# Layer 1 of a two-layer transformer kernel: KV times the gated output weights, z on the queries, gate and spread matrices on GpSimd

## The reference

```python
Q = relu(proj(Wq, bq)) * decay        # decay = exp(-pos / n)
K = relu(proj(Wk, bk)) * decay
V = proj(Wv, bv)
KV = einsum('bhnd,bhne->bhde', K, V)  # 32 x 32 for each head
Ksum = K.sum(axis=2)
Z = 1.0 / (einsum('bhnd,bhd->bhn', Q, Ksum)[..., None] + EPS)
out = einsum('bhnd,bhde->bhne', Q, KV) * Z
x = x + ga * (out @ Wo.T + bo)
```

## Time and profile before

| | |
|---|---|
| time, median of 3 runs | 2087.24 us (2083.95 to 2090.82) |
| profiled execution, its own time | 2086.4 us |
| its span | 2084.5 us |
| PE busy | 1964.7 us, 94% |
| DVE busy | 1078.9 us, 52% |
| ACT busy | 639.0 us, 31% |
| POOL busy | 439.6 us, 21% |
| mean granted clock | 0.976 |

### The profile page before, as it was taken

How to read it: one execution, slowest core, us unless ns; L and a number is a source line. 1 busy time by engine, 2 the same in 40 slices (tenths; PEclk the granted TensorE clock), 3 DMA queues, 4 the chain that set the end, 5 groups by cost and what they waited for, 6 DMA issues and landing times. The chain is left out here.

```text
span 2084.5 us, 25631 instructions
## 1 busy us (share of the span) xinstructions
PE 1964.7 (94%) x10088; PEld 1399.4 (67%) x10088; DVE 1078.9 (52%) x1876; ACT 639.0 (31%) x1152; POOL 439.6 (21%) x385
## 2 busy tenths in 40 slices
PE   6999999999999997699999999997998969999998
PEld 4677545554545545578888888886885658888886
DVE  4456876666766715743434434336335665434334
ACT  3231445455555563322111111113221231111111
POOL 0122766666544365000000000000003000000000
PEclk9999999999999999899999999999999989999999
DMA  9753421422421003020000000002000011100002
GB/s 316 227 154 115 93 52 42 93 56 49 108 47 29 5 2 132 23 74 31 31 1 31 31 31 1 1 1 89 6 6 31 1 41 41 31 21 21 6 0 81
DMA packets 61720, 111.86 MB, mean 54 GB/s; under 512 B 6000, under 2 KB 21248, under 8 KB 61568
## 3 DMA queue, kind: packets, MB, share of 16 engines
q1 hardware_dynamic: 54144, 85.05, 14.2%
q0 software_dynamic: 7456, 25.18, 4.0%
HBM read 84.77 MB, written 25.44 MB: 53 GB/s over the span
## 5 line engine op out<-in xcount | busy, mean ns | idle before, releaser
L446 DVE TENSOR_REDUCE part_max<-banks 128x1 f32<-128x512 f32 (+2 forms) x640 | 357.3, 613 | 156.4 <-PE banks L418 96.6
L917 ACT ACTIVATE probs<-banks 128x512 f32<-128x512 f32 (+3 forms) x640 | 310.7, 538 | 282.7 <-PE banks L844 141.1
L418 PE MATMUL banks<-kst,qst 96*128 96x512 f32 (+2 forms) x640 | 261.6, 417 | 12.1 <-DVE part_max L446 9.2
L840 PE MATMUL banks<-qst,kst 98*128 98x512 f32 (+2 forms) x640 | 251.7, 413 | 0.2 <-ACT probs L917 0.2
L1384 DVE TENSOR_TENSOR tokens_a<-banks,tokens_a 128x512 f32<-128x512 f32 x224 | 151.5, 688 | 73.5 <-PE banks L210 71.9
L1409 DVE TENSOR_TENSOR tokens_b<-banks,tokens_b 128x512 f32<-128x512 f32 x64 | 44.3, 692 | 267.6 <-ACT tokens_b L1330 267.6
L208 PE MATMUL banks<-h_hi,f_wg_hi 128*128 128x512 f32 x432 | 170.4, 394 | 12.4 <-DVE f_wg_lo L1348 12.4
L208 PE MATMUL banks<-f_d_hi,f_hid_hi 128*128 128x512 f32 x432 | 171.7, 398 | 5.9 <-issue 3.6
L209 PE MATMUL banks<-h_lo,f_wg_hi 128*128 128x512 f32 x432 | 170.1, 394 | 0.0
L210 PE MATMUL banks<-f_d_hi,f_hid_lo 128*128 128x512 f32 x432 | 169.9, 393 | 0.0
L210 PE MATMUL banks<-h_hi,f_wg_lo 128*128 128x512 f32 x432 | 169.7, 393 | 0.0
(11 more groups left out here) (188 smaller groups left out, 3268.7 us busy)
## 6 DMA issues: line engine op xcount, KB each, us to landing
tokens_a<-in_L_wmod SPq DMA_DIRECT2D x12, 1024.0 KB, 7.1
qst<-q_hi SPq DMA_DIRECT2D x32, 256.0 KB, 6.0
kst<-k_hi SPq DMA_DIRECT2D x32, 256.0 KB, 8.1
x<-in_L_attn_x SPq DMA_DIRECT2D x4, 1024.0 KB, 13.2
q_hi<-qk_out_hi POOLq DMA_DIRECT2D x16, 256.0 KB, 3.0
q_lo<-qk_out_lo POOLq DMA_DIRECT2D x16, 256.0 KB, 3.4
k_hi<-qk_out_hi POOLq DMA_DIRECT2D x16, 256.0 KB, 4.1
k_lo<-qk_out_lo POOLq DMA_DIRECT2D x16, 256.0 KB, 4.4
```

The costliest lines, as they stand in the source:

```text
L418: mm = nc.tensor.matmul(dst[:, 0:wide], qst[n % QS][0:BIASROW, h, P * t:P * t + P], kst[(NB * g + c) % KS][0:BIASROW, h, 0:wide], start=Tr ...
L446: nc.vector.tensor_reduce(part_max[:, n % 2, ht, c:c + 1], max_bank(slot)[:, 0:wide], AX_X, ALU.max).then_inc(max_read, 1)
L840: mm = nc.tensor.matmul(dst[:, c0:512], kst[ck % KS][0:BIASROW + 2, h, at:at + P], qst[n % QS][0:BIASROW + 2, h, c0:512], start=True, stop ...
L917: nc.scalar.activation(probs[:, q % PS, h, c0:512], score_bank(sh)[:, c0:512], ACT.Exp, scale=SCALE).then_inc(exp_done, 1)
```

## The change

The output weights are gated by POOL, at the end of its list in the QKV block, once both loads have landed. In the next block kv is transposed by PE (4 transposes into bank 6) and copied by ACT, and each of its four tiles is multiplied with a chunk of the gated weights (4 plain fp32 matmuls into banks 2 to 5). These merged weights are split into w_hi (ACT) and w_lo (DVE). The spreads of z then multiply the queries themselves, and the projection of the scaled queries with the merged weights gives the attention output. The 16 numerators and their 16 copies are gone, and so are DVE's four gate multiplications. The four spread matrices are made by POOL, ahead of its bias additions. DVE makes the first w_lo after z and the other three after the fourth attend.

```diff
             gated = sem(ctx, tag + "w_gated_s")
...
+            merged = sem(ctx, tag + "merged")
...
+                def bias_vector(dve):
+                    dve.wait_ge(bias_loaded, 16)
+                    nc.vector.tensor_tensor(bias_row[:], bias_row[:], gate, ALU.mult).then_inc(bias_gated, 1)
+
+                def merged_tensor(pe, k, left):
+                    nc.tensor.matmul(bank[2 + k][:], left, raw[:, k, :], start=True, stop=True).then_inc(merged, 1)
+
+                def merged_scalar(act):
+                    for k in range(KT):
+                        act.wait_ge(merged, k + 1)
+                        nc.scalar.copy(w_hi[:, k, :], bank[2 + k][:]).then_inc(w_hi_s, 1)
+
+                def merged_vector(dve, ks):
+                    for k in ks:
+                        dve.wait_ge(w_hi_s, k + 1)
+                        nc.vector.tensor_tensor(w_lo[:, k, :], bank[2 + k][:], w_hi[:, k, :], ALU.subtract).then_inc(w_ready, 1)
...
# the QKV block, POOL, after its four w_lo
+                        pool.wait_ge(early_loaded, OUT1)
+                        for k in range(KT):
+                            nc.gpsimd.tensor_tensor(early_square[:, k, :], early_square[:, k, :], early_gate[:], ALU.mult)
...
# the output-projection block
+                def zb_bank(i):
+                    return bank[6 + i % 2][:]
                 def zb_step(pe, i):
                     b, g = divmod(i, G)
-                    dst = use_bank(pe, ("zb", i))
                     if i == 0:
                         pe.wait_ge(z_step, 4)
                         pe.wait_ge(spread_ready, NB)
+                    elif i >= 2:
+                        pe.wait_ge(at_ready, i - 1)
...
                 def attend(dve, i):
                     b, g = divmod(i, G)
                     dve.wait_ge(zb_mm, i + 1)
-                    dve.wait_ge(num_copied, i + 1)
                     here = at[:, g, 512 * b:512 * b + 512]
-                    nc.vector.tensor_tensor(here, bank_of(("zb", i)), here, ALU.mult).then_inc(at_ready, 1)
+                    nc.vector.tensor_tensor(here, zb_bank(i), here, ALU.mult).then_inc(at_ready, 1)
...
# POOL
+                        pool.wait_ge(spread_loaded, 32)
+                        for b in range(NB):
+                            nc.gpsimd.tensor_scalar(spread[:, b, :], pattern, of_block[:, b:b + 1], None,
+                                                    ALU.mult).then_inc(spread_ready, 1)
                         out_p.bias_gpsimd(pool)
...
# PE
+                        for g in range(G):
+                            last = nc.tensor.transpose(bank[6][:, P * g:P * g + P], kv[:, g, :], ident[:])
+                        last.then_inc(kv_turned, 1)
                         for g in range(G):
                             for b in range(NB):
...
                         last.then_inc(den_mm, 1)
-                        for kind, i in events[:G * (NB + 1)]:
...
+                        for g in range(G):
+                            if g == 0:
+                                pe.wait_ge(kv_copied, 1)
+                            out_p.merged_tensor(pe, g, kv_t[:, P * g:P * g + P])
+                        for i in range(G):
+                            zb_step(pe, i)
                         on_tensor(pe)
...
# ACT
-                        out_p.weights_scalar(act)
-                        for i in range(G * FIRST):
-                            numerator(i)
-                        for i in range(G * FIRST, G * NB):
-                            numerator(i)
+                        act.wait_ge(kv_turned, 1)
+                        nc.scalar.copy(kv_t, bank[6][:]).then_inc(kv_copied, 1)
+                        out_p.merged_scalar(act)
                         out_p.hi_scalar(act, 0)
                         on_scalar(act)
...
# DVE
-                        out_p.weights_vector(dve)
-                        dve.wait_ge(spread_loaded, 32)
-                        for b in range(NB):
-                            nc.vector.tensor_scalar(spread[:, b, :], pattern, of_block[:, b:b + 1], None,
-                                                    ALU.mult).then_inc(spread_ready, 1)
+                        out_p.bias_vector(dve)
                         dve.wait_ge(den_mm, 1)
...
+                        out_p.merged_vector(dve, range(0, 1))
                         for i in range(G):
                             attend(dve, i)
+                        out_p.merged_vector(dve, range(1, KT))
                         out_p.lo_vector(dve, 0)
```

More of the change, by code:

```diff
@@ L1695, in build_program @@
                 z_step = sem(ctx, "z_step")
-                num_mm = sem(ctx, "num_mm")
-                num_copied = sem(ctx, "num_copied")
+                kv_turned = sem(ctx, "kv_turned")
+                kv_copied = sem(ctx, "kv_copied")
                 zb_mm = sem(ctx, "zb_mm")
@@ L1704, in build_program @@
                             mod_cols[:, 1, CB, :], h2_hi, h2_lo, zbufs=1)
[L1707 to L1710, removed]
+                pattern, z_sum, kv_t = (norm.z[:, 0, i, :] for i in range(3))
+                def zb_bank(i):
+                    return bank[6 + i % 2][:]
                 def zb_step(pe, i):
                     b, g = divmod(i, G)
-                    dst = use_bank(pe, ("zb", i))
                     if i == 0:
@@ L1718, in zb_step @@
                         pe.wait_ge(spread_ready, NB)
[L1719 to L1733, removed]
+                    elif i >= 2:
+                        pe.wait_ge(at_ready, i - 1)
+                    nc.tensor.matmul(zb_bank(i), spread[:, b, P * g:P * g + P], z_hi[:], start=True, stop=False)
+                    nc.tensor.matmul(zb_bank(i), spread[:, b, P * g:P * g + P], z_lo[:], start=False, stop=True).then_inc(zb_mm, 1)
                 def attend(dve, i):
@@ L1782, in _ @@
                     def _(act):
-                        def numerator(i):
-                            b, g = divmod(i, G)
-                            act.wait_ge(num_mm, i + 1)
-                            nc.scalar.copy(at[:, g, 512 * b:512 * b + 512], bank_of(("num", i))).then_inc(num_copied, 1)
-                        out_p.weights_scalar(act)
-                        for i in range(G * FIRST):
-                            numerator(i)
-                        for i in range(G * FIRST, G * NB):
-                            numerator(i)
+                        act.wait_ge(kv_turned, 1)
+                        nc.scalar.copy(kv_t, bank[6][:]).then_inc(kv_copied, 1)
+                        out_p.merged_scalar(act)
                         out_p.hi_scalar(act, 0)
@@ L1809, in _ @@
                         nc.vector.tensor_tensor(z_lo[:], z_sum, z_hi[:], ALU.subtract).then_inc(z_step, 1)
+                        out_p.merged_vector(dve, range(0, 1))
                         for i in range(G):
                             attend(dve, i)
+                        out_p.merged_vector(dve, range(1, KT))
                         out_p.lo_vector(dve, 0)
-                        dve.wait_ge(spread_ready, NB)
-                        dve.wait_ge(z_step, 4)
                         on_vector(dve)
```

## The result

The changed kernel takes 2069.85 us (median of four, 2068.76 to 2072.13) against 2086.12 beside it: ratio 0.992, 95% interval 0.9901 to 0.994. Run again on another occasion it gave 0.9932 (0.9918 to 0.9945). So it is 0.7 to 0.8% faster, some 14 to 16 us. The forecast was 6.6 us, and the range ended 4 us short of the result: the sign was right, the size was not. One execution ran apart, the profiled one of e7 (2385.81 us at a mean granted clock of 0.77 from beginning to end), and is left out of every comparison.

What follows compares the result with a forecast made beforehand. PE bounds long stretches of the QKV block and after 1760; at the output-projection start engines wait for each other. -10.4 there and +3.8 in the QKV block give -6.6 on 2086.4: 2079.8, median forecast 2080.6 us, range 2074.0 to 2088.5.

Steps and rivals of the forecast that it cites:

- Where the gain is made: Output-projection block: first projection, held by late z, numerators and ACT's order, starts at 1614.0 against 1624.38, gaining 10.4 us.
- point 2: Output-projection block: z starts at 1598.8, not 1602.39, keeps its 6.84 us beside POOL and is complete at 1605.6.
- point 1: Output-projection block: transposes ahead of the denominators move their end later by 0.5 us (0.4 to 1.0), to 1598.7.
- the loss in the QKV block: POOL's gate multiplications hold DVE 4.3 us; 3.2 reach PE, plus 0.6 for the clock: 3.8 us lost (0 to 6).
- Points 3 and 4: Output-projection block: four merged products (3.7 us) cost nothing; POOL's spreads, 1.3 us each, end at 1602.3, 3.3 in hand.
- Point 5: Output-projection block: first spread matmul to end of fourth attend takes 4.5 us (3.9 to 5.2), ending at 1610.2.
- Point 6: Output-projection block: w_lo until 1612.0, then c_lo 1.2 us plus 0.65 lost to POOL; the product starts at 1614.0.
- The cover of 1.07 us on ACT: QKV block: slack between the first key tile's end at 1450.26 and L182 on ACT at 1451.33, taken off DVE's delay.
- The 0.6 us for a falling clock: QKV block: 0.6 us added because PE's clock may fall after its 3.2 us standstill.
- the question of proportion or turns: QKV block: DVE slowed in proportion beside POOL (3.0 us lost) or held for whole POOL instructions (4.3 taken).
- Rival C: Output-projection block: POOL's spread matrices set the start; deciding from 2.1 us each, 0.3% slower (2093.6) at 5.4; chance 0.08.
- its lowest case: Gate multiplications don't reach PE and the output-projection gain is at its 11.6 us bound: 2075.6, with run spread 2074.0.

Runs made afterwards that it cites:

- e7: Changed kernel with POOL's four gate multiplications taking one input (a gate column; weights not gated rightly): 2072.13 us, ratio 0.9931, three executions.
- the square: Block start to first projection: before 32.4 us, merged weights alone (e2) 26.8, spreads on POOL alone with additions held back (e6) 26.8, both (changed kernel) 18.3.
- e2: Changed kernel with the four spread matrices made by DVE again: 2079.28 us, ratio 0.9963.
- e3: Kernel before with one part of the change alone, the four spread matrices made by POOL: 2082.76 us, ratio 0.9989, not told from no change.
- e4: Changed kernel with POOL's four gate multiplications held back until the items of two token blocks have been read: 2072.83 us, ratio 0.9938.
- e7b: The kernel of e7 run again for an undisturbed profile: 2071.15 us, ratio 0.993.
- e8: e1 with the bias gated and added to x by POOL in the QKV block, behind the items DVE has read: 2068.76 us, ratio 0.9917.
- e1: Changed kernel with the output weights gated by DVE at the start of the output-projection block, not by POOL in the QKV block: 2071.12 us, ratio 0.993.
- a2: The changed kernel itself run once more: 2071.45 us, ratio 0.9932.
- e6: e3 with POOL's bias additions held back until the second c_lo is done: 2078.32 us, ratio 0.9961.
- e9: e8 with eleven matmuls nobody reads, one ahead of the first spread and ten ahead of the first projection: 2068.10 us, ratio 0.9914.
- e8b: The kernel of e8 run again, on the same chip as a2: 2069.31 us, ratio 0.9925.

## Why the prediction was right or wrong

**Where the gain is made** was right: the first projection hung on the late z, the numerators and ACT's order, and the square shows that the first two carry 14.1 us together. What failed is the price of three terms: the length of z (point 2), its start (point 1) and the loss in the QKV block.

**Point 1, the denominators.** I moved their end by 0.5 us to a later time; it came earlier. z started 5.75 us after the block's start, not 6.8. The same 16 calls took 3.64 (e2) to 6.23 us (e3), by how long the clock was at 0.50 in them; in e2 it stayed at 1.00. It goes with the length of the QKV block: where that was 173.2 or 173.3 us the denominators took 3.6 to 4.65 us, where it was 170.7 to 171.2 us they took 5.0 to 6.2 (13 profiles). So some 1.2 us of what POOL's gates cost PE came back as clock: the denominators ended 5.7 us after the block's start, and 6.9 in e4, e7b and e8. With the longer z this is why e4 won nothing. In e1 they ended only 0.2 us later than in the changed kernel; there it was z, the spreads and c_lo. That the two are linked is seen in all these profiles; why is not shown.

**Point 2, the length of z**, is the step that failed, with the largest error of the block. I kept 6.84 us "since POOL works beside it as before"; it took 5.27, 1.6 us less. The 6.84 holds only if POOL's additions are beside z's last two instructions, the cast and the rest. By my figures they would have been: spreads done 10.3 us after the block's start, the cast at 10.9. In fact the spreads cost 1.55 each on POOL, not 1.3, and ended at 10.8, and z, early, had its last two instructions from 9.9 to 11.0. Both errors were needed for it: either alone leaves an addition beside one of the two at the least. In e1 and e4, where the additions began before z_lo, z took 6.6 and 6.4.

**Points 3 and 4**: the merged products cost nothing, and the spreads were done at 1604.03, before z was complete at 1604.22. That was luck to 0.2 us, as I gave them 3.3 us in hand.

**Point 5, the spreads and attends**, was sized for a low clock (4.5 us) that did not come: from 1604.27 to 1606.55 + 1.29 = 1607.84 are 3.6. In a2 the clock did fall in them and they took 4.1. **Point 6**: 3.6 us from the fourth attend to the projection against 3.8 forecast. The first c_lo took 1.84 us, as forecast (1.85), but e3 shows that the bound was wrong: a starved c_lo took 7.14 us. It wasn't in my range at all and would have cost 5 us.

These terms sum up the 3.7 us between 22.0 and 18.3: 1.05 + 1.6 + 0.9 + 0.2.

**The QKV block** was forecast at +3.8 us and took +2.1. The mechanism was right, and e1, e4 and e7b bear it out: POOL delays DVE, and DVE's late z delays L182 on ACT and so PE. The term that was too large is DVE's delay, and a part that I added was not there. The two w_lo and the decay products lost 2.0 + 0.8 us, and the L195 ahead of them 1.0, which I hadn't counted; z ended 3.65 us later (counted from the block's first transposes, 1427.99 before and 1427.07 after), not 4.3. The cover of 1.07 us on ACT held: L182 came 2.49 us later, 1.2 less than z. PE lost it in three places, 1.07 at L195, 0.77 and 0.5 at the transposes, not in one idle of 3 us. The 0.6 us for a falling clock did not come. Some 0.3 us came back between the blocks, where PE's wait fell from 2.73 to 2.39; so it did in e4, whose QKV block of 170.7 us puts the price of the gates at 2.5 us. Why that wait is shorter is not shown.

On the question of proportion or turns, where I cited the Trainium skill's page "SBUF — State Buffer", section "Who interferes with whom": the 3.65 us lie between the 3.0 and the 4.3 of the two ways, and do not decide it. The times of e3 agree with a port that is held for whole instructions. They disagree with the page's rule that whoever issues first gets it, since four additions that started after c_lo had begun its 7.14 us went ahead of it; here the measurement decides.

**Rival C** did not come: 1.55 us each is below the 2.1 from which it decides. But with z complete at 11.0 us and the pattern there at 4.6, it would have decided from 1.6 on. The Trainium skill's "GPSIMD Engine Reference", section "4.1 Engine selection", led the other way: one-input work was dearer than the two-input addition (1.27), not cheaper.

**The rest** of the 14.2 us between the spans, and of the 16.3 between the medians, lies in stages that the change didn't touch, and the range left it out. The feed-forward part took 375.9 to 378.2 us over these kernels. In all of them PE stands still for 2.21 us once near its end, and in some the clock falls behind that. Stretches of the 11 us behind it, before and then after (length, PE busy, clock, DMA share, GB/s):

```profile
2043.09:2054.09 11.00, 11.00 (x41) 0.84 0.01 1
```

```profile
2031.60:2042.60 11.00, 11.00 (x48) 1.00 0.01 1
```

41 matmuls against 48 are 7 x 0.23 = 1.6 us. e6 and e9 look like after there, e3, e8 and a2 like before; as a2 is the changed kernel itself, this is no effect of the change. In the stage from the first projection on, a2 and after, the same kernel, differ by 2.5 us. And the code ahead of the QKV block, the same in all, ended between 1417.1 and 1421.0. The touched stages alone, 14.1 - 2.1 = 12.0 us, give 2087.24 - 12.0 = 2075.2, which lies inside the range. My range had 1.6 us for the scatter of the runs below its lowest case; 5.4 were due: 2.2 in the untouched stages, 2.3 as the profiled execution after is the slowest of its four (2072.13 against a median of 2069.85), and 0.8 as the one before is below the median that I counted from.

## What to carry to other kernels

Ask of every VectorE step that moves what GpSimd does beside it in its new place, and take its duration from a row with the same neighbour, not from its own row in another company. A long train of two-input instructions on GpSimd should start behind, or be spaced out around, VectorE's two-input instructions on the critical path; one wait was worth 6 us of the stage (e6 against e3, one profile each). When two chains are late for the same point, removing either shows less than half of what removing both does, so a part measured alone says little.

## What the runs showed of the hardware

A VectorE instruction with two SBUF inputs (1.21 us alone) took 7.14 us beside a gapless train of GpSimd additions that took 1.26 to 1.295 each: it can lose every turn. In other kernels the same pair shared: 1.34 to 2.33 us for a c_lo beside additions of up to 2.28 (a2, e2, after, e1). What decides between the two is not shown. GpSimd's one-input multiplications of 128 x 512 took 1.55 us, more than its two-input additions; beside them VectorE's two w_lo lost 0.65 us, beside two-input ones 2.0. Ten matmuls of 0.23 us whose results nobody reads, in an idle gap of 2.2 us (e8b), together with one more in the gap ahead of the spreads, kept the clock at 1.00 and gave back 1.6 us in the work behind it (e9 against e8b, one profile each).
